# GpSimd's gathers wait until the last pair but one has landed

## The reference

```python
q = (feats @ Wq.T + bq).reshape(bs, NHEAD, HDIM).transpose(1, 0, 2)   # k, v alike
r, c = (edge_index[:, 0], edge_index[:, 1])          # source, destination
sim = jnp.einsum('hed,hed->eh', q[:, c, :], k[:, r, :]) * scale
m = jax.ops.segment_max(sim, c, num_segments=bs)
p = jnp.exp(sim - m[c])
s = jax.ops.segment_sum(p, c, num_segments=bs)
out_e = (p / s[c]).T[..., None] * v[:, r, :]
agg = jax.ops.segment_sum(out_e.transpose(1, 0, 2).reshape(-1, NHEAD * HDIM), c, num_segments=bs)
return agg @ Wo.T + bo
```

## Time and profile before

| | |
|---|---|
| three executions | 1725.07, 1727.82, 1732.25 us |
| median | 1727.82 us |
| profiled execution | 1727.49 us, of it the span 1725.8 us |
| busy in the span | PE 1058.0, DVE 972.2, POOL 538.4, ACT 432.9 us |
| GpSimd's DMA queue | 39872 packets, 117.67 MB, 24.9% of the 16 engines' span |

### The profile page before, as it was taken

One profiled execution on the slowest core, in us unless ns is written; L12 is line 12 of the kernel. 1 busy time (PEld: TensorE's weight loads), 2 busy tenths in 40 slices (PEclk: granted clock), 3 DMA queues, 4 the chain that ended last, 5 costly groups with the idle time before them and its releaser, 6 DMA issues. The chain is left out here.

```text
span 1725.8 us, 20777 instructions
## 1 busy us (share of the span) xinstructions
PE 1058.0 (61%) x4059; PEld 687.7 (40%) x4060; DVE 972.2 (56%) x2394; ACT 432.9 (25%) x1253; POOL 538.4 (31%) x608
## 2 busy tenths in 40 slices
PE   0489483655666556565656655565668709999950
PEld 0255251433343333343334333343335605666630
DVE  5479865667666666667666666666777400000016
ACT  1222251322222222222222222222232402212111
POOL 1234425333334344343333444333300060000024
PEclk9999765777677677668776777667789558999985
DMA  4622404443444444444334444444300231323214
GB/s 142 112 92 65 125 14 122 117 119 111 112 124 125 115 133 130 121 124 122 111 111 122 130 131 131 125 117 129 99 1 0 73 107 51 126 94 128 87 39 122
DMA packets 86446, 179.36 MB, mean 104 GB/s; under 512 B 14979, under 2 KB 51909, under 8 KB 86413
## 3 DMA queue, kind: packets, MB, share of 16 engines
q0 software_dynamic: 39872, 117.67, 24.9%
q1 hardware_dynamic: 42125, 57.30, 10.5%
q10 hardware_dynamic: 4416, 4.01, 0.7%
HBM read 157.65 MB, written 21.63 MB: 104 GB/s over the span
## 5 line engine op out<-in xcount | busy, mean ns | idle before, releaser
L1099 PE MATMUL at_pa<-at_pv,at_hot 128*125 128x264 f32 x832 | 321.5, 532 | 229.3 <-DVE agg L973 160.3
L1099 PEld LDWEIGHTS at_pa<-at_pv,at_hot 128*125 128x125 f32 x832 | 193.3, 253 | 329.5 <-issue 256.9
L1042 PE MATMUL at_pq<-q,at_hotT 125*128 x1248 | 232.7, 330 | 79.5 <-DVE at_prod L981 56.9
L845 POOL DMA_INDIRECT slot<-kv_d,idx x192 | 183.5, 956 | 294.9 <-ACT idx L854 239.7
L845 POOL DMA_INDIRECT at_slot<-kv_d,idx x192 | 183.4, 955 | 289.7 <-ACT idx L854 236.9
L1042 PEld LDWEIGHTS at_pq<-q,at_hotT 125*128 125x128 bf16 x1248 | 142.5, 114 | 165.4 <-issue 112.0
L973 DVE TENSOR_TENSOR agg<-agg,at_pa 125x264 f32 x416 | 176.4, 424 | 33.5 <-remote 6.8
L1436 DVE TENSOR_TENSOR yb<-xp,b 128x256 f32<-128x256 f32 (+1 forms) x32 | 13.6, 425 | 269.5 <-PE xp L1467 269.5
L1016 DVE TENSOR_TENSOR at_pv<-at_slot,at_pp 128x528 f32<-128x528 f32 x104 | 71.8, 700 | 125.0 <-remote 91.8
L1016 DVE TENSOR_TENSOR at_pv<-slot,at_pp 128x528 f32<-128x528 f32 x104 | 71.7, 700 | 121.4 <-remote 87.0
L902 DVE TENSOR_REDUCE at_sc<-at_prod 128x16 f32<-128x512 f32 x208 | 139.2, 670 | 0.0
(11 more groups left out here) (295 smaller groups left out, 1408.4 us busy)
## 6 DMA issues: line engine op xcount, KB each, us to landing
slot<-in_w SPq DMA_DIRECT2D x16, 1024.0 KB, 7.5
at_locrow<-loc_d SPq DMA_DIRECT2D x26, 500.0 KB
slots_d<-slot SPq DMA_DIRECT2D x7, 512.0 KB
kv_d<-vst SPq DMA_DIRECT2D x25, 128.9 KB
base<-in_x SPq DMA_DIRECT2D x5, 625.0 KB
kv_d<-kst SPq DMA_DIRECT2D x25, 125.0 KB
slot<-kv_d,idx POOLq DMA_INDIRECT x192
at_slot<-kv_d,idx POOLq DMA_INDIRECT x192
```

Of the source, the lines that this page charges most:

```text
L845: pool.indirect_dma_start(slot[par][:, u, :], None, m.kv_d, bass.IndirectOffsetOnAxis(ap=m.idx[:, par, u:u + 1].bitcast(U32), axis=0)).the ...
L1042: mm = pe.matmul(pq[j % 2][:, (u % 2) * D:(u % 2 + 1) * D], hotT[:, u, :], at(m.q3, window)[:, part, :], start=(part == 0), stop=(part == 2))
L1099: mm = pe.matmul(pa[u % 4][:, 0:H * VW], hot[:, u % 8, :], pv[:, u % 4, :, :].rearrange("p h c -> p (h c)"), start=True, stop=True)
```

## The change

Ahead of the first gather of a pair, from the third pair of a chunk on, GpSimd waits until the pair two before it has landed, by that pair's `arrived` semaphore. At most four gathers of a chunk can then be in flight.

```diff
                                 pool.wait_ge(S.pv_made, U * k + U // 2 * par + u // 2 + 2 - U)
                                 pool.nop(nofuse=True)
+                            if u % 2 == 0 and u >= 4:
+
+                                pool.wait_ge(S.arrived[par * 8 + u // 2 - 2], 32 * k + 32)
+                                pool.nop(nofuse=True)
                             pool.indirect_dma_start(slot[par][:, u, :], None, m.kv_d,
```

## The result

The changed kernel takes 1710.86 us (median of four runs, 1703.87 to 1712.21), the kernel before 1728.41 us (four runs, 1725.07 to 1732.25). The ratio is 0.989, its 95% interval 0.9855 to 0.9924: faster by 17.5 us. The forecast was 1619.5. The direction was right, the size was six times too large. The profiled execution took 1711.66 us, its span is 1709.9.

A forecast was written before the change was run, and what follows sets the result against it. It took TensorE's signals, held while gathers are in flight, as the bound. A chunk saves 6.7 us less 2.2 of residual holds, 4.5; over 24 chunks 108 us, so 1727.5 - 108 = 1619.5 us, range 1567 to 1768.

The forecast's parts named there:

- The bound and what it costs: Attention stage: late TensorE signals, not the gathers' data, bound it; gathers in flight cost 8.4 us a chunk, some 200 us.
- the hold: Ahead of VectorE's line 1016: TensorE's signals come up to 8 us late while GpSimd's gathers are in flight.
- The cost of one wait: GpSimd's gathers: third pair starts at 5.8 us, gaps of 0.75 us ahead of each run of four, twelfth gather at 15.4.
- Signals pass in the gaps: Likeliest case, chance 0.50: gaps between runs of four let TensorE's signals through, eighth product near 8.5 us; 1567 to 1670 us.
- the list of signs: What would show the likeliest case, among them line 1016's seventh and eighth product before 14 us, chunks 32 to 36 apart.
- The gathers then bind: Line 981 then needs the last gather, landed at 24.8 us; a chunk is no shorter than 32.1, 6.7 below 38.8.
- four residual holds of 1.1 us: Each run of four gathers can hold signals only from 5.8 to 6.9 us; half of this, 2.2 us, on the path.
- The evidence I had misread: Chunk at 554.31: second gather 1.3 us late, seventh product at 7.14 without a hold; read as signals passing after a pause.
- the hold moves: Rival, chance 0.08: early signals freed, later ones held, at line 973 or 981; 4.5 us a chunk, 108 us slower, 1835.
- The slower rival: Chance 0.24: signals go only when the whole row of gathers is over; eighth product 1.5 us later a chunk, 1745 to 1770.
- the free wait: Rival, chance 0.15: each wait is over before GpSimd comes to it, so no gap that matters; 1715 to 1733 us.

The follow-up runs named there:

- e7_pool_plain: Kernel before with GpSimd's gathers replaced, on its own queue, by plain loads of 128 neighbouring table rows: 1521.8 us.
- e5_pause: Kernel before plus, ahead of the 5th, 9th and 13th gather, a landing wait, four small memsets and a wait for them: 1601.1 us, ratio 0.927.
- narrow gathers: Kernel before with gathers of 32 bytes a row instead of 2080, as many gathers and rows: 1730.06 us (before 1727.76).
- e14_565_long: Kernel before plus two pauses of about 1.4 us, ahead of the 6th and 12th gather: 1582.8 us on a chip where the kernel before takes 1519.83.
- e16_one_long: Kernel before plus one pause (landing wait, six memsets) ahead of the 9th gather: 1584.88 us on a chip where the kernel before takes 1519.83.
- memset alone: Kernel before plus one small memset ahead of the 5th, 9th and 13th gather, waiting only for the memset before: 1739.2 us (before 1733.79).
- half gathers: Kernel before with gathers of 64 rows instead of 128, as many gathers: 1745.64 us (before 1733.79).
- e19_five_third: Kernel before plus one small memset, waited for, ahead of the 4th, 7th, 10th, 12th and 14th gather: 1604.19 us, ratio 0.930.
- e6_fours: The change with its waits ahead of the 5th, 9th and 13th gather only: 1722.61 us, ratio 0.998 to the kernel before.

## Why the prediction was wrong in size

- **The bound and what it costs**: right. I put the hold at some 200 us; without it the kernel takes 1520 to 1522 us, 206 to 208 less than with it on the same chip, by plain loads. Its chunk of 30.4 us without the hold is that of e7_pool_plain (30.0 to 30.9 in all but one).
- **The cost of one wait**: right in sum, in part by luck. I had 5.8 us for the third pair within 5.3 to 6.3; it starts 5.5 to 5.9 after the first gather, in all chunks but one. The twelfth gather goes out at 15.4 (median; 15.4 forecast), the last at 21.4 on average (21.2). But the pauses ahead of the 5th, 9th and 13th gather are 0.60, 0.51 and 0.43 us (medians) where I had 0.75, and the waits ahead of the 7th, 11th and 15th, which I had free, take 0.12, 0.28 and 0.28 though they are as good as met: 2.2 us in all, as forecast. On the landing time, in the chunk at 706.11: from the second gather to the third pair pass 4.27 us (5.53 - 1.26), and from the end of what is waited for to a gather 0.78 (the memsets and the ninth gather of e5_pause), which leaves 3.5 us.
- **Signals pass in the gaps**: in part. The eighth product moved from 16.8 to 10.5 us, not to 8.5; before 14 it was in 23 of 24 chunks, as the list of signs asked.
- **The gathers then bind**: not reached. My bound was 32.1 us a chunk; with the landing as measured where the gathers do bind (4.1 to 4.2 us, 22.0 to the last product at 26.2) it is 32.7. Line 985 has no wait for the DMA that matters in the changed kernel, and chunks are 38.3 us apart.
- **The step that failed** is the term "of the four residual holds of 1.1 us I put half on the path, 2.2". I had reasoned that each run of four starts afresh and holds at most to the end of its own packets. It doesn't: a pause of 0.6 us leaves the hold standing, and the hold doesn't go by packets at all (the narrow gathers). The row copy comes at 20.8 us where 12.9 is free, 7.9 us late, in ten chunks only when the whole row of sixteen is over, and the chunk ends 5.6 us above the bound of 32.7. The 6.4 us gained at the eighth product are 1.8 at the row copy and 0.7 at the chunk's end: 0.7 x 24 = 17 us, the measured gain.
- **The evidence I had misread** was the chunk at 554. I took its seventh product as proof that a pause lets the row start anew. The same rows show sums held for 6.8 us later in that chunk. That was the rival "the hold moves", to which I gave 0.08, and its mechanism and its sign ("remote" grows ahead of the sums and the score products) are what happened: the sixteen gathers now stand in one row, with the chain's row copy waiting at its end. Only its price (+4.5 us a chunk) came from one extreme chunk; the two effects almost cancel.
- **The slower rival and the free wait** are out: the eighth product no longer follows the end of the gathers, and the pauses are there.

That a hold of this kind can be missing on a chip was in none of my cases. On such a chip the change should cost what its pauses cost: the last gather goes out 2.5 us later than in an unbroken row (21.4 against 18.9), and at the 2.6 to 3.0 us paid there for 3 us of pauses that is, as an estimate, 50 to 60 us. It wasn't run there.

**What stays open.** Why a gather holds TensorE's signals at all; whether the indices or the time GpSimd is occupied decides, since plain loads differ in both (on the two chips without the hold the gathers are issued every 1.26 us too, so that time alone doesn't make it); why two of six chips (of the experiments) don't show it, or whether it is a passing state of theirs; and the exact rest that is needed: e14_565_long and e16_one_long never met a chip with the hold.

The record allows an estimate of how the hold grows. It is arithmetic on measured times; no run was made to test it, and none shows what would lie behind it. Behind a row of twelve gathers the eighth product starts 16.9 to 17.3 us after the first gather in nearly every chunk of four kernels (before, narrow, half, memset alone), whether the twelfth went out at 13.9 or, with half gathers, at 13.4; and the seventh product of the kernel before starts in 20 of 24 chunks at 8.5, 9.9 or 11.3. These are about 12, 6, 7 and 8 times 1.41 us. If each gather holds the signals for 1.41 us from the first one's start on, with one issued every 1.26, the hold grows by 0.15 us a gather. Four gathers with a pause of 0.6 us take 5.65 us, just what four times 1.41 make, so nothing is left over for the signals; a pause of 1.0 us leaves 0.4. Sixteen then hold them for 22.6 us, and the ten late row copies of the changed kernel come at 23.0 to 23.2. By this estimate a third of a microsecond is worth 121 us because 0.6 us only just makes up for what four gathers add, and a pause ahead of the second gather is wasted because one gather has added only 0.15.

**A version faster than both** is e5_pause, 1601 us where the kernel before takes 1728 (7.3% less), and e19_five_third is nearly as good. But either gains only where the hold is: on the two chips without it the kernel before is faster by 4% than the five short pauses, and e5_pause, with the same idle time, was not run there.

## What to carry to other kernels

When an engine waits for "remote" while the producer's record has long ended, look at what GpSimd is issuing at that time, and test with the same bytes from another queue: here that one run put a price of 208 us on it. A hold that is lifted at one consumer can fall on the next signal in the row, as here, so follow the chain to the next iteration's first instruction before multiplying a gain at one place by the number of iterations. And run a version tuned against such an effect on more than one chip, for the same pause was worth 7% on one and cost 4% on another.

## What the runs showed of the hardware

- With GpSimd issuing an indirect gather every 1.26 us, signals of TensorE's instructions arrive up to 8.3 us after the instruction's end in the records, from about 7 us into the row until some time after the last gather's issue: 2.0 to 2.2 us in the changed kernel, 3.1 behind the twelve of the kernel before, 3.6 in its chunk at 554.31, 3.6 to 3.8 behind twelve half gathers. VectorE's signals aren't late: where ScalarE's index copy had to wait, it mostly starts 0.12 to 0.14 us after the product that it waits for, in both kernels.
- It depends on neither bytes (32 or 2080 a row: 1730.06 and 1727.76 us) nor rows (64 or 128: 1745.64 and 1733.79, within the spread), and is as good as absent ("remote" 3.0 and 3.7 us) with plain loads of the same bytes from SyncE or GpSimd (1521.4 and 1521.8 us).
- Some 3 us of rest for GpSimd over a chunk's sixteen gathers clear most of it, in three pauses or in five (1601 and 1604 us); 2.0 to 2.6 us clear little (1711 to 1767 us), and 1.3 us ahead of the second gather don't let the row copy through (20.0, 24.1 and 25.5 us after the first gather in the chunks near 550 us of the changed kernel, of e6_fours and of the kernel before).
- Two of six chips don't show it: the same kernel takes 1520 and 1521 us there, and 1728 to 1734 on the four others.
- A semaphore wait of GpSimd's that is already met costs 0.1 to 0.3 us ahead of a gather, one that ends late 0.78 us from its release to the gather (behind the memsets of e5_pause).
